# Edge stage of a four-layer graph network: the gathers' row numbers copied four blocks ahead and first in VectorE's step, and waits that other waits imply left out

## The reference

```
src, dst = (edge_index[0], edge_index[1])
m_input  = concatenate([x[src], x[dst], edge_attr_64], axis=-1)      # 128 + 128 + 64
h        = relu(m_input @ W1 + b1)
messages = relu(h @ W2 + b2)
agg      = segment_sum(messages, dst, num_segments=3125)
updated  = x + relu(agg @ Wn + bn)          # then a layer norm with gamma and beta
```

## Time and profile before

| | us |
|---|---|
| median of three runs | 1897.14 |
| the profiled execution, its own time | 1896.5 |
| its span in the trace | 1894.7 |
| edge stage on POOL, first to last gather | 611.0 to 1623.6 |
| TensorE busy in the span | 1607.5 (85%) |
| GpSimd busy in the span | 762.5 (40%) |
| mean granted clock of TensorE | 0.947 of full speed |

### The profile page before, as it was taken

One profiled execution on the slowest core, in us unless ns is written; L12 is line 12 of the kernel. 1 busy time (PEld: TensorE's weight loads), 2 busy tenths in 40 slices (PEclk: granted clock), 3 DMA queues, 4 the chain that ended last, 5 costly groups with the idle time before them and its releaser, 6 DMA issues.

```text
span 1894.7 us, 35263 instructions
## 1 busy us (share of the span) xinstructions
PE 1607.5 (85%) x10288; PEld 1047.9 (55%) x10289; DVE 761.5 (40%) x2772; ACT 704.0 (37%) x1406; POOL 762.5 (40%) x798
## 2 busy tenths in 40 slices
PE   2777777998997888889998998999899999572996
PEld 1444445454546566666676666667666666431444
DVE  7998894112224322233233334323333333276004
ACT  4666664002001344454445444444544444302001
POOL 3000000000000677777776777777777777200000
PEclk9999996999998899999998999999999899885998
DMA  1000000001003333333333333333323233000001
GB/s 55 0 0 0 0 0 3 1 1 39 1 0 104 105 81 81 82 80 82 80 80 80 80 82 80 81 80 80 81 77 83 79 78 81 24 5 2 1 0 35
DMA packets 158371, 94.01 MB, mean 50 GB/s; under 512 B 120529, under 2 KB 143824, under 8 KB 158296
## 3 DMA queue, kind: packets, MB, share of 16 engines
q0 software_dynamic: 25088, 51.43, 9.5%
q1 hardware_dynamic: 133208, 41.60, 9.0%
HBM read 86.44 MB, written 6.52 MB: 49 GB/s over the span
## 4 chain that ended last, share of the span: by engine, by line
PE 25%; POOL 17%; issue 13%; DVE 6%; DMA 5%; ACT 2%; SPq 1%; DVEq 0%; POOLq 0%; ACTq 0%
POOL arena L669 17%; PE ps L788 6%; PE ps L907 4%; PE ps L917 4%; PE ps L900 3%; DMA arena<-x_w1a,idx 3%; PE ps L887 2%; PE ps L896 2%; PE ps L925 1%; DVE arena L1506 1%; PE ps L966 1%; DMA arena<-in_edge_attr 1%; DVE stats L1496 1%; DMA x_w1b<-arena 1%; DVE arena L1516 0%
## 5 line engine op out<-in xcount | busy, mean ns | idle before, releaser
L669 POOL DMA_INDIRECT arena<-x_w1a,idx x784 | 743.6, 948 | 860.3 <-issue 828.5
L788 PE MATMUL ps<-adj,arena 128*128 (+2 forms) x1575 | 315.6, 362 | 14.8 <-DVE arena L1471 8.1
L1646 DVE TENSOR_TENSOR arena<-win_i,drel 128x96 f32<-128x96 f32 x196 | 50.8, 259 | 497.0 <-PE ps L917 492.9
L788 PEld LDWEIGHTS ps<-adj,arena 128*128 128x128 bf16 x1575 | 146.1, 99 | 178.8 <-issue 28.1
L907 PE MATMUL ps<-w_c,arena 128*128 128x128 f32 x1568 | 230.8, 291 | 0.0
L1215 ACT ACTIVATE arena<-ps 88x512 f32<-88x512 f32 x196 | 115.8, 591 | 299.3 <-PE ps L887 295.5
L722 PE MATMUL ps<-arena 128*128 128x300 bf16 x784 | 165.0, 296 | 63.3 <-DVE arena L1458 63.3
L907 PEld LDWEIGHTS ps<-w_c,arena 128*128 128x128 f32 x1568 | 193.2, 194 | 41.2 <-issue 41.2
L917 PE MATMUL ps<-arena 128*24 128x128 f32 x1568 | 211.8, 279 | 2.2 <-ACT arena L1224 2.2
L900 PE MATMUL ps<-arena 88*128 88x512 f32 x392 | 206.3, 608 | 0.0
L1113 ACT ACTIVATE adj<-ps 128x300 f32 x392 | 166.7, 449 | 97.6 <-PE ps L727 91.9
(11 more groups left out here) (163 smaller groups left out, 1353.0 us busy)
## 6 DMA issues: line engine op xcount, KB each, us to landing
arena<-in_edge_attr SPq DMA_DIRECT2D x196, 128.0 KB
arena<-x_w1a,idx POOLq DMA_INDIRECT x784
arena<-x_w1b SPq DMA_DIRECT2D x196, 12.0 KB
x_spill<-arena SPq DMA_DIRECT2D x1, 1600.0 KB, 7.7
x_w1a<-arena SPq DMA_DIRECT2D x6, 256.0 KB, 2.3
x_w1b<-arena SPq DMA_DIRECT2D x6, 256.0 KB, 2.7
arena<-x_spill SPq DMA_DIRECT2D x6, 256.0 KB, 2.7
out_x<-arena SPq DMA_DIRECT2D x3, 512.0 KB
```

The lines of the kernel that those rows point to most:

```text
L669: pool.indirect_dma_start(out=z_e[v][:, j * D:(j + 1) * D], out_offset=None, in_=xa_d[:, :], in_offset=bass.IndirectOffsetOnAxis(ap=idx[:, ...
L788: last = pe.matmul(ps[:, u, 0:w], parts[q][:, k, :], adj[:, k, bass.ds(c0, w)], start=(k == 0 and q == 0), stop=(k == NT - 1 and q == 2))
```

## The change

Three things are changed, all in the edge stage.

1. VectorE's `step(i, v)` now begins with `gather_index(*at(i, v + SLOTS))`, so the row numbers of block b + 4 are copied before `add_window`, where those of block b + 3 were copied after it. Step 0, which had no copy, has one. The last full step asks for row 196, so `src_idx` is one row longer and that row is zeroed once in the preparation.
2. On TensorE six waits are left out of the steady step: for `ect_out` of the block before in `inputs_t`, for `h_ready` two back in `hidden_t`, for `h_ready` and `m_sum` in `messages`, and for `oh_e_ready` and `sums_out` in `sum_nodes`.
3. ScalarE drops `z_ready` in `hidden_relu` and `win_ready` in `take_sums`. VectorE drops `ec_used` in `block_start` and `sums_ready` in `add_bias`. Where a first step needs such a wait, `first=True` keeps it.

```
-        src_idx = sb("src_idx", [P, NB, J], I32)
+        src_idx = sb("src_idx", [P, NB + 1, J], I32)
...
-            def inputs_t(i, v):
+            def inputs_t(i, v, first=False):
                 passed(pe, ec_loaded, i, v, by=16)
                 passed(pe, ec_onehot, i, v)
-                passed(pe, ect_out, i, v, back=1)
+                if first:
+                    passed(pe, ect_out, i, v, back=1)
...
             def hidden_t(i, v):
                 z_t = ps[:, 2 + v % 2, :]
-                passed(pe, h_ready, i, v, back=2)
                 passed(pe, g_loaded, i, v, by=64)
...
-            def messages(i, v):
-                passed(pe, h_ready, i, v)
-                passed(pe, m_sum, i, v, back=1)
+            def messages(i, v, first=False):
+                if first:
+                    passed(pe, h_ready, i, v)
...
                 passed(pe, msg_ready, i, v)
-                passed(pe, oh_e_ready, i, v)
-                passed(pe, sums_out, i, v, back=1)
...
-            def hidden_relu(i, v):
-                passed(act, z_ready, i, v)
+            def hidden_relu(i, v, first=False):
+                if first:
+                    passed(act, z_ready, i, v)
...
                 passed(act, sums_ready, i, v)
-                passed(act, win_ready, i, v, back=1)
...
+            dve.memset(src_idx[:, NB, :], 0)
...
-                passed(dve, ec_used, i, v, back=2)
+                if first:
+                    passed(dve, ec_used, i, v, back=2)
...
                 passed(dve, m_ready, i, v)
-                passed(dve, sums_ready, i, v, back=1)
...
             def step(i, v, b=None, left=3, first=False):
 
+                if left >= 3:
+                    gather_index(*at(i, v + SLOTS))
                 if b is not None:
                     add_window(*at(i, v - 2), b)
                 if left >= 3:
-                    if not first:
-                        gather_index(*at(i, v + 3))
-                    block_start(*at(i, v + 3))
+                    block_start(*at(i, v + 3), first)
                 add_bias(i, v)
```

More of the change, by code:

```diff
@@ L935, in step @@
                     sum_nodes(*at(i, v - 1))
-                messages(i, v)
+                messages(i, v, first)
                 if not first:
@@ L974, in _ @@
             with pe.Else():
-                inputs_t(0, 0)
-                inputs_t(0, 1)
+                inputs_t(0, 0, first=True)
+                inputs_t(0, 1, first=True)
                 hidden_t(0, 0)
@@ L1277, in _ @@
                 inputs_out(0, 1)
-                hidden_relu(0, 0)
+                hidden_relu(0, 0, first=True)
                 step(0, 0, first=True)
@@ L1638, in _, with block_start @@
             base_regs = [dve.alloc_register(f"dve_base{v}") for v in range(SLOTS)]
-            def block_start(i, v):
-                passed(dve, ec_used, i, v, back=2)
+            def block_start(i, v, first=False):
+                if first:
+                    passed(dve, ec_used, i, v, back=2)
                 passed(dve, sums_ready, i, v, back=SLOTS)
@@ L1749, in _ @@
                 for v in range(3):
-                    block_start(0, v)
+                    block_start(0, v, first=True)
                 dve.memset(agg_all, 0.0).then_inc(agg_zero, 1)
```

## The result

The changed kernel takes 1878.92 us, the median of four runs (1875.68 to 1881.83). The kernel before, run beside it, takes 1900.10 us (1894.93 to 1903.61, four runs). The ratio is 0.989, with a 95% interval of 0.9857 to 0.9923: it is faster, by about 1.1%. The profiled execution took 1880.53 us with a span of 1878.7 us; that of before had a span of 1894.7, so 16.0 us went. The forecast was 1880 us and 16.6 us, worked out on a profiled execution; the two medians are 21.2 us apart. What follows takes the 16.0 us of the two traces apart, each of one execution. Ratios in this document are taken over the runs within 1.5% of the fastest of their kernel.

A forecast was written before the change was run, and what follows sets the result against it. No engine is full; in the edge stage's plain turns POOL (20.0 us) and TensorE (19.64 us) are nearly equally loaded. Gains of 3.5 + 13.1 = 16.6 us off 1896.5 give 1879.9, so 1880 us, range 1867 to 1890.

The forecast's parts named there:

- The start: First blocks of the edge stage: POOL's two pauses for the copy of row numbers go, 1.9 + 1.6 = 3.5 us gained.
- The plain turns: Plain turns of the five segments: POOL's added lead removes TensorE's 28 waits for gathered rows, 13.1 us gained.
- The five gather waits of the update turns: Update turns: five waits of about 1.7 us, 8.4 us, vanish but bring nothing; TensorE waits 4.3 us for features.
- The clock: Granted clock around the five update turns: the longer feature wait could cost from -5 to +12 us; taken as 0.
- Rival C: Update turns: one wait of 4.3 us replaces two, longer low clock; 1886 us, far end 1892; chance 0.13.
- The waits left out: Edge stage, TensorE, ScalarE and VectorE: leaving waits out gains 0; bounds on TensorE nothing or 15.8 us.
- Rival B: Edge stage: the waits do cost on TensorE, so leaving them out gains another 15.8 us, 1864 us; chance 0.08.
- E: Edge stage steps: longer `src_idx` moves buffers behind it, TensorE's passes reading them slow, 0.16 us a step; 1905 us; chance 0.05.
- D: Update turns: another limit holds POOL, its lead isn't built, only the start is gained; 1893 us; chance 0.11.

## Why the prediction was right, point by point

The measured median, 1878.92 us, lies 1 us from the forecast of 1880 and inside its range of 1867 to 1890. The path to it was mostly, not wholly, as foretold.

**The start, forecast 3.5 us, measured 4.3 us over blocks 0 to 11.** As forecast, both pauses of the earlier trace rows are gone and the waits of the earlier trace rows stay (21.2, now 17.9 us). The size is the two pauses and some tenths more.

**The plain turns, forecast 13.1 us, measured 15.0 us.** All 28 waits of the earlier trace rows are gone, turns are 19.60 us as forecast, and POOL had the lead. The term was too small because the sum of waits shown is not all that lateness costs: before, blocks 112 and 115 took 5.56 and 5.41 us with 0.29 and 0 us of gather wait shown, and take 5.10 and 5.16 now. The difference of whole steps is the better measure.

**The five gather waits of the update turns, forecast 0, measured as part of a loss of 3.4 us.** This is the term that was off. The mechanism held up to the wait itself: the gather wait (1.63 in the earlier trace rows) is gone, the features come when they did (in sum over the five turns 50.6 us after the start of the block with the gather wait, now 50.4), and one wait of 4.1 to 4.4 us stands there in the last four update turns, forecast 4.3. In the first, 0.67 us of gather wait is left beside 3.64 us. But I took "nothing" to be the end of it, and the 3.6 us are lost behind the wait. The block behind took 8.39, 9.56, 8.34, 9.49 and 9.69 us before and takes 10.56, 10.21, 11.13, 10.75 and 10.73 now: 7.9 us more, with 8.4 us of waits gone ahead of it. Another 1.63 us each is lost in blocks 109, 141 and 173 (5.92 in place of 4.29), where the clock falls a second time (0.50 from 1174 to 1177 us in the first of them); smaller gains elsewhere in these turns leave -3.4.

**The clock, forecast 0 within -5 and +12 us.** The time at the lower level is the same, 44.1 against 44.3 us, and yet 3.4 us were lost in these turns. The forecast's formula takes the lower level as half of the full one, and that is what the trace of before shows, 1.00 and 0.50. But the measure was the wrong one, for it counts all low time alike. In three of the five turns before, the clock fell already at the work between the two waits, as in the rows of the same turn above; what that work lost, the wait for the features was shorter by, 1.4 to 1.6 us in place of 2.6 to 2.7. Now the clock falls within the one wait (at 1160.1 us in the turn shown, 1.8 us before its end), and what is low behind it falls on work that no wait makes up for (L915 1.90, L907 2.08). That is 36.2 us of work at the lower clock in place of 29.9; half of the difference, 3.2 us, is nearly the whole loss, and 0.7 us comes from the waits for ScalarE behind it. The copy alone had 34.6 us of such work and lost 3.8. There is one trace of the kernel before and its low stretches differ from turn to turn, so the size is less sure than the sign. Rival C had a price of 6 us for this, and about half of that came. Behind each of the four waits of 4.1 to 4.4 us, and behind that of 3.64, the work starts at a granted clock of 0.50: L888 takes 1.08 us in all five, and 0.60 in a plain turn.

**The waits left out, forecast 0.** Right on the short chips: the copy alone has the same plain turn of 19.60 us with all waits in place and 0.9871 of the time. On a long chip they make 0.9999 alone, but 18.3 us together with the early copy. Rival B (15.8 us) falls. E falls with the turn of 19.60 us, which is no longer than the 19.64 worked out for TensorE before; D is refuted by the stretches without a wait.

The sum came out as 16.0 us where 16.6 was forecast because two terms that were too small (0.8 and 1.9 us) nearly cancel one of 3.4 us that was left out. So the nearness of the total is partly luck; and it is a nearness of two single executions, where the medians are 21.2 us apart with an interval of some 6 us to either side.

What the prediction did not consider is the chip. Its gain holds where the kernel before takes 1897 to 1901 us. On three others, with 2277 to 2300 us, the copy alone is slower by 0.9 to 1.2%, and the whole change, run on one of the three, shows no gain. Nothing in the trace of before could have shown it, since that trace has no late signal.

**What stays open.** Why TensorE's signals are late on the long chips. For unbroken rows of gathers as the cause speak the counts by position (179 late, 8 not), the readers that went on after POOL had stopped, and the fall of late signals with two blocks ahead. Against it speak the 38 of 41 signals that were not late at the fifth or a later gather there, and the third of the late ones that were raised within a row. The runs that should have forced it fell on short chips, where the traces show no late signal in rows of any length (each within 0.02 us before, after and with the copy alone). A rival was not tested: the long-chip traces also lack over half of the DMAs' semaphore updates, so recording the trace may itself be slow there, and every time here comes from an execution that has a span and a clock from the profiler. Whether a pause of some tenths of a microsecond would pay on a long chip is not known.

## What to carry to other kernels

Where two engines have nearly the same load (19.64 and 20.0 us a turn here), an earlier hand-over of four small numbers can be worth a per cent: it lets the engine with bursts of slack (here POOL in the update turns) save it for the turns that are tight. Leaving out waits that other waits imply brought nothing that the short-chip runs can see; where signals come late, and with the early copy, it brought 18 us, so it is worth a run of its own. When two waits merge into one, count what the clock does to the work behind the longer one (29.9 us of it at 0.50 became 36.2 here), not only whether the waits add up. And such a change is measured on more than one chip: the sign of the early copy turned.

## What the runs showed of the hardware that I had not expected

- On three chips TensorE's signals reached the other engines late in the edge stage (285 of 851 over 1 us in the whole change, the latest 9.1 us in the waits alone), and the kernel before took 20% longer there. Nearly all of this time lies in the edge stage: behind the last gather's start the waits alone took 275.0 us on such a chip, the kernel before 272.1 on a short one. Outside the edge stage no such lateness shows, and the gathers began at 608.7 to 610.2 us, on short chips at 610.0 to 611.0. In the profile this has no line of its own: it appears as idle time "remote" on the readers, and as 17 to 20% of the chain under "another core or an unknown queue" (1% with two blocks ahead), though the kernel runs on one core.
- A gather of 128 rows has the same pitch of 1.25 us on both kinds of chip (a median of 0.94 to 0.95 us each, and 0.30 us behind it; twelve in a row from 1207.81 to 1221.54 us on a long one); so it is not their issue that is slower there, but what POOL and TensorE wait for.
- In this kernel two short waits with work between them cost less than one wait of the same sum, since in three of the five turns the clock fell between them: 29.9 us of work at 0.50 behind the wait for the features became 36.2, with 44.3 and 44.1 us of low time in all.
- From the start of a block's last gather until POOL could go on with all four landed passed 3.2 us (1209.23 to 1212.44 us, with the pause at the head).
